# Early second norm, and one up-projection of the next chunk ahead of the output projection, in a fused transformer block

## The chip, the cores and the metric

One Trainium2 chip (trn2), of which the kernel uses one core. The metric is the device time of one execution in microseconds (us). Three executions of the kernel before took 955.98, 957.22 and 959.0 us, median 957.22.

## What is computed

A transformer block with adaptive norms on x of shape 8 x 1024 x 256 (8 rows, 1024 tokens, 256 channels), all in float32:

```python
mod = (silu(c) @ wmod).reshape(8, 6, 1, -1)      # sa, ca, ga, sb, cb, gb; ga and gb kept from small values
h = layernorm(x) * (1 + ca) + sa
x = x + ga * attention(h, W_in, W_out)           # 16 heads of 16; Chebyshev orders 0 to 5 of q and k
h = layernorm(x) * (1 + cb) + sb
x = x + gb * ffn(h)                              # shared expert + 2 of 8 experts, hidden size 128
```

The attention is linear: for each order, the Chebyshev polynomial of k times v is summed over all earlier tokens (a prefix sum), multiplied by the polynomial of q, weighted and added up; the sum is divided by the same quantity without v. The feed-forward computes all 8 routed experts for all tokens and weights each expert's hidden values by its combine weight, sqrt(softplus(logit)) of the two best experts and zero elsewhere; the shared expert has weight one.

## The kernel before

The work is cut into 16 chunks of 512 tokens, two (p = 0, 1) for each of the 8 rows i. It is a software pipeline over 18 steps. In an ordinary step for chunk c, the kernel does the attention of c, the projections (k, q, v) of c+1 (`nxt`), the second norm and the routing of c-1 (`prev`), the experts of c-2 (`exp`), and the first norm's statistics of c+2. Steps 0 and 1 have no experts (step 0 no second norm either); the last four drop parts one by one. Prefix sums are carried from p = 0 to p = 1.

Each engine has its own program, written out by hand in a `step` function; the order of the calls there is the order of execution, and semaphores with fixed counts tie the engines together. Whoever stands in front of a wait holds up all that is behind it on its engine. A "half" is one of six blocks of 128 output columns (k0, k1, q0, q1, v0, v1).

- **TensorE** (L1503): up-projections of the experts (`expert_up`, L1462; 6 matmuls each, in `split_product`, L1368, since weights and inputs are split into a high and a low part), down-projections (`expert_down`, L1487; they add up in `acc`), the six projections of the next chunk, transposes of the norms' results (`transposes`, L1348, matmuls L1359; n = 0 the first norm, n = 1 the second), routing logits (L1394) and their transposes by token (L1402), head sums (L1421), denominators (L1434), the output projection (`project_out`, L1438, matmuls L1445) and, last in the step, the transposes of the combine weights (L1457, L1459). Up-projections and projections go through a ring of two PSUM banks: a group may start when the group two places ahead has been copied out, so for q0 that is k0, and for q1 it is k1. `tr` is two further banks that transposes, head sums and the output projection share.
- **ScalarE** (L863): copies out of the ring, for an expert with a SiLU (`silu(e)`, L845), for k, q and v with a bias (`copy`, L800); `highs` (L781, the high part n1H or n2H from `tr`); the second norm's scaling in four operations (`normalise_second`, L429, operation L435), the squares of the polynomials (L817, L820), `scale_even` (L828, L829), sums for the first norm, the logits' copy (L852) and the copies of the combine weights (L860, L861).
- **VectorE** (L1191): `residual` (L1096, reads `tr`), `token_stats` (L378), `lows` (L961, the low part n1L or n2L from `tr`), the odd orders (L984, L986), `weigh` (the orders times v, L1002 to L1008), `prefix` (scans, L1021), `order_product` (L1042, L1046), `weigh_hidden` (L1169), top-2 and softplus, denominators, `divide` (L1088) and the gated output (L1178).
- **GpSimd** (L738): `inv_std` (ten small operations, L353 to L366, that turn the statistics into scale and shift of the norm), `weigh_order_5` (L653), `scale_wo` (L723, W_out times the row's gate, once per row, at p = 0), additions of orders by accumulating DMAs (L665), two small chains for routing, and the output's DMA (L714).
- **SyncE** (L600): loads, the spread of combine weights and inverse denominators over the partitions by way of DRAM, stores, and the loads of the gates (`load_gate`, L568; 0 the gate of the attention, 1 that of the feed-forward).

In steps without the first norm of the next chunk, and in steps without experts, the calls concerned are left out and the rest keeps its order. The wait ahead of a ring group, in `expert_up` and `project`:

```python
at, bank = use[f"e{e}"]
pe.wait_ge(ring_copied, at - 1)
```

## Time and profile before

| what | value |
|---|---|
| median of 3 runs (lowest, highest) | 957.22 us (955.98, 959.0) |
| the profiled execution: time, span | 953.07 us, 951.3 us |
| TensorE busy (share of the span), instructions | 860.2 us (90%), 4377 |
| TensorE weight loads | 648.6 us (68%), 4377 |
| VectorE | 815.7 us (86%), 1263 |
| ScalarE | 489.8 us (51%), 860 |
| GpSimd | 408.3 us (43%), 502 |
| weightings of hidden values (L1169), 128 | 111.1 us, mean 870 ns |
| mean granted clock of TensorE | 0.964 |

The profiled execution is one of its own, and its 953.07 us are to be set beside its span of 951.3 us; the runs are other executions. "Busy" counts the time in which an engine has an instruction in work. Consecutive matmuls overlap, so a row's own duration is longer than its step to the next row; where the length of a group matters, the starts of two rows are subtracted. The granted clock is the share of TensorE's full clock (2.4 GHz) that it was given. In the rows below PE is TensorE, DVE VectorE, ACT ScalarE, POOL GpSimd. At a row's end, in brackets, stands the idle time ahead of it and what ended it. `x8` is the number of instructions in a row; one matmul in float32 shows as two.

### The profile page before, as it was taken

The page shows a single profiled execution, that of the slowest core. Times are in us where ns is not written, and L with a number is a line of the kernel's source. Part 1 is how long each engine was busy: PE and PEld are TensorE (multiplying, and loading weights), DVE is VectorE, ACT ScalarE, POOL GpSimd, SP SyncE. Part 2 cuts the span into 40 slices and gives each one's busy share as a digit, 9 for nine tenths or more (in the row PEclk, how much of TensorE's full clock was granted, in tenths as well). Part 3 has the DMA queues.
Part 4 walks back from the last instruction along what each step waited for, and adds up shares of the span by engine and source line. Part 5 has one row for each costly group of instructions (what it writes and reads, how often), then busy time and mean ns, then how long its engine had stood idle before and what let it go on. Part 6 is the DMA issues. An engine that isn't in the chain of part 4 may idle for free. (4 is left out here: it accounts for less than half of the span.)

```text
span 951.3 us, 14272 instructions
## 1 busy us (share of the span) xinstructions
PE 860.2 (90%) x4377; PEld 648.6 (68%) x4377; DVE 815.7 (86%) x1263; ACT 489.8 (51%) x860; POOL 408.3 (43%) x502
## 2 busy tenths in 40 slices
PE   5766739999999999999999999999999999979998
PEld 4545427676767676786767676777767676756786
DVE  2696979999989998999989998999999998889423
ACT  4634546555556656655656566566556563441321
POOL 2341444363636355453636254543646253463220
PEclk9975769999999999999999999999999999999999
DMA  8014134453533535453534445354634243443422
GB/s 309 1 29 89 45 68 145 86 153 76 137 92 77 153 79 160 86 155 70 153 77 96 130 87 165 68 155 90 162 71 133 66 100 113 78 133 83 117 79 55
DMA packets 51705, 100.34 MB, mean 105 GB/s; under 512 B 5380, under 2 KB 34127, under 8 KB 49623
## 3 DMA queue, kind: packets, MB, share of 16 engines
q1 hardware_dynamic: 36356, 66.14, 21.2%
q0 software_dynamic: 14832, 33.03, 20.2%
q10 hardware_dynamic: 482, 0.74, 0.2%
q8 instruction: 18, 0.29, 0.1%
q14 instruction: 17, 0.13, 0.0%
HBM read 57.68 MB, written 17.06 MB: 79 GB/s over the span
## 5 line engine op out<-in xcount | busy, mean ns | idle before, releaser
L1487 PE MATMUL acc<-w,hid 128*128 128x256 f32 x1128 | 262.5, 380 | 2.6 <-DVE hid L1169 2.6
L1487 PEld LDWEIGHTS acc<-w,hid 128*128 128x128 f32 x1128 | 213.9, 190 | 37.6 <-DVE hid L1169 4.7
L845 ACT ACTIVATE hid<-ring,b1row 128x512 f32<-128x512 f32 x144 | 98.7, 685 | 143.0 <-PE ring L1368 140.4
L1169 DVE TENSOR_TENSOR hid<-hid,cfw 128x512 f32<-128x512 f32 x128 | 111.1, 870 | 37.0 <-DMA cfw<-cf_rows 21.6
L665 POOL DMA_DIRECT2D feat<-feat x48 | 43.7, 910 | 228.8 <-DVE feat L1046 115.0
L800 ACT ACTIVATE feat<-ring,bqkv 128x512 f32<-128x512 f32 x96 | 65.7, 686 | 81.9 <-PE ring L1368 81.9
L1368 PE MATMUL ring<-n2H,w1H 128*128 128x512 f32 x288 | 102.5, 437 | 0.0
L1445 PE MATMUL tr<-wo_g,feat 128*128 128x256 f32 x256 | 65.3, 413 | 35.9 <-DVE feat L1088 35.9
L1021 DVE TENSOR_TENSOR_SCAN feat<-zero,carry,feat 128x512 f32<-128x512 f32 x80 | 97.1, 1261 | 0.0
L1021 DVE TENSOR_TENSOR_SCAN feat<-zero,feat 128x512 f32<-128x512 f32 x80 | 95.7, 1243 | 0.0
L1368 PE MATMUL ring<-n2H,w1L 128*128 128x512 f32 x288 | 90.8, 397 | 0.0
L1368 PE MATMUL ring<-n2L,w1H 128*128 128x512 f32 x288 | 90.5, 395 | 0.0
L1421 PE MATMUL tr<-feat,const 128*32 128x512 f32 x640 | 89.1, 602 | 0.0
L1445 PEld LDWEIGHTS tr<-wo_g,feat 128*128 128x128 f32 x256 | 51.6, 207 | 49.2 <-DVE feat L1088 33.7
L1368 PE MATMUL ring<-n1H,winH 128*128 128x512 f32 x192 | 69.5, 444 | 15.2 <-issue 7.9
L820 ACT ACTIVATE feat<-feat,const 128x1024 f32<-128x1024 f32 x64 | 70.2, 1142 | 1.0
L353 POOL TENSOR_TENSOR ms<-stats 128x4 f32<-128x4 f32 x18 | 30.2, 1678 | 88.4 <-DVE stats L378 88.4
L1368 PEld LDWEIGHTS ring<-n2H,w1L 128*128 128x128 f32 x288 | 54.4, 189 | 12.7
L1368 PEld LDWEIGHTS ring<-n2L,w1H 128*128 128x128 f32 x288 | 54.5, 189 | 12.5
L1368 PE MATMUL ring<-n1H,winL 128*128 128x512 f32 x192 | 62.8, 409 | 0.0
L1368 PE MATMUL ring<-n1L,winH 128*128 128x512 f32 x192 | 62.8, 409 | 0.0
L1368 PEld LDWEIGHTS ring<-n2H,w1H 128*128 128x128 f32 x288 | 48.8, 191 | 18.5 <-issue 11.7
(171 smaller groups left out, 1559.8 us busy)
## 6 DMA issues: line engine op xcount, KB each, us to landing
feat<-feat POOLq DMA_DIRECT2D x48, 512.0 KB, 4.6
cfw<-cf_rows SPq DMA_DIRECT2D x16, 1280.0 KB, 7.6
xin<-in_L_attn_x SPq DMA_DIRECT2D x16, 512.0 KB, 9.3
feat<-inv_rows SPq DMA_DIRECT2D x32, 256.0 KB
cfw<-cf_rows SPq DMA_DIRECT2D x16, 512.0 KB, 3.6
out<-x SPq DMA_DIRECT2D x15, 512.0 KB, 8.5
out<-fin POOLq DMA_DIRECT2D x15, 512.0 KB, 6.0
cfw<-cf_rows SPq DMA_DIRECT2D x16, 256.0 KB, 4.5
```

Source lines behind the costliest of these rows:

```text
L353: nc.gpsimd.tensor_tensor(t(1), m0, m1, ALU.subtract).then_inc(mv_steps[n], 1)
L665: g.dma_start(f(into), f(of), accum_op=ALU.add).then_inc(added[n], 16)
L800: a.activation(feat[:, (K0 + p, Q0 + p, V0)[m // 2], m % 2], ring[bank][:, :], ACT.Identity, bias=col(bqkv[:, (2, 3, 0, 1, 4, 5)[m]], i)). ...
L820: a.activation(f((qa, qb)[which - 1]), f(s), ACT.Square, bias=cv["biases"][:, which - 1:which]).then_inc(squares, 1)
L845: a.activation(hid[:, e % NG], ring[bank][:, :], ACT.Silu, bias=b1row[:, e:e + 1]).then_inc(ring_copied, 1)
L1021: last = v.tensor_tensor_scan(feat[:, W + n, h], zero[:, 0:1].to_broadcast([P, CT]), feat[:, W + n, h], carry[:, n, h:h + 1] if p else 0.0 ...
L1169: v.tensor_tensor(hid[:, e % NG], hid[:, e % NG], cfw[:, (e - 1) % NW], ALU.mult).then_inc(hidw_ready, 1)
L1368: last = mm(out, w, x, start=(n == 0), stop=(n == len(terms) - 1))
L1421: last = mm(tr[q][g_ * QS:(g_ + 1) * QS, :], cv["headsum"][:, (r // HPH) * QS:(r // HPH + 1) * QS], feat[:, srcs[n], h], start=(n < 4 and ...
L1445: last = mm(tr[t // 2][:, (t % 2) * D:(t % 2 + 1) * D], attn[:, k, t * P:(t + 1) * P], wo_g[:, k], start=(k == 0), stop=(k == KD - 1))
L1487: last = mm(acc[t // 2][:, t % 2], hid[:, e % NG, t * P:(t + 1) * P], w2[:, e], start=False, stop=(e == E), skip_group_check=True)
```

## The change

The second norm of chunk c-1 moves towards the head of the step, on all engines:

- VectorE aggregates its own statistics (`second_mean_var`: four `bn_aggr`, variance plus epsilon, negative mean), and GpSimd has two operations left (`second_inv_std`: power -1/2, product) in place of ten.
- ScalarE normalises in four operations behind n1H and ahead of the SiLUs of experts 1 and 2, takes n2H behind these, and copies q1 apart from k0, k1 and q0, behind the logits.
- TensorE transposes the first norm directly at the step's head (now waiting for the residual's halves one by one), the second norm behind the down-projection of expert 0; the logits stand behind q0, their transposes behind q1, and expert 1 behind that.
- VectorE takes n1L directly behind the aggregations, n2L behind the second weighting, and the third weighting behind the second prefix sum. GpSimd's `weigh_order_5` waits for the second weighting as well.
- The up-projection of the next step's expert 0 stands ahead of the output projection, behind the last down-projection.
- SyncE loads the attention's gate for row i+1 at the end of row i, ahead of the last spread of weights.

```diff
@@ -134,6 +134,7 @@
...
         stats = sb("stats", [P, 2, NT, 6])
+        mean_var = sb("mean_var", [P, NT, 2])
         ms = sb("ms", [P, 2, 12, NT])
@@ -221,6 +222,8 @@
...
         var_steps = sem("variance_steps")
+        aggregate_begun, aggregated, mean_var_ready, second_pow = (
+            sem(f"second_{n}") for n in ("aggregate_begun", "aggregated", "mean_var", "pow"))
         sums_begun, squares_begun, norm_begun = (sem(f"{n}_begun") for n in ("token_sums", "token_squares", "normalisation"))
@@ -378,6 +381,27 @@
...
 
+        def second_mean_var(dve, i, p):
+
+            c = number(i, p)
+            dve.wait_ge(stats_ready[1], c + 1)
+            dve.sem_inc(aggregate_begun, 1)
+            for t in range(NT):
+                last = nc.vector.bn_aggr(mean_var[:, t], stats[:, 1, t])
+            last.then_inc(aggregated, 1)
+            dve.wait_ge(aggregated, c + 1)
+            nc.vector.tensor_scalar(ms[:, 1, 8], mean_var[:, :, 1], EPS_LN, None, ALU.add).then_inc(mean_var_ready, 1)
+            nc.vector.tensor_scalar(ms[:, 1, 10], mean_var[:, :, 0], -1.0, None, ALU.mult).then_inc(mean_var_ready, 1)
+
+        def second_inv_std(pool, i, p):
+
+            c = number(i, p)
+            pool.wait_ge(mean_var_ready, 2 * c + 2)
+            ge(pool, norm_ready[1], c)
+            nc.gpsimd.tensor_tensor(ms[:, 1, 9], ms[:, 1, 8], k_("-half", NT), ALU.pow).then_inc(second_pow, 1)
+            pool.wait_ge(second_pow, c + 1)
+            nc.gpsimd.tensor_tensor(ms[:, 1, 11], ms[:, 1, 10], ms[:, 1, 9], ALU.mult).then_inc(rstd_ready[1], 1)
+
         def token_sums(act, i, p):
@@ -599,9 +623,8 @@
...
                 if p == 0:
-                    if loads or i < B:
-                        ge(sp, wo_ready, i)
-                        load_gate(i, 0)
+                    if i == 0:
+                        load_gate(0, 0)
                     if gb:
@@ -613,6 +636,9 @@
...
                     load(sp, i + 2, p)
+                if p == CB - 1 and i + 1 < B:
+                    sp.wait_ge(wo_ready, i + 1)
+                    load_gate(i + 1, 0)
                 if number(i, p) and number(i, p) <= CB * B:
@@ -650,6 +676,7 @@
...
                 ge(pool, numerator, c)
+                pool.wait_ge(weighted, (ND - 1) * c + 2)
                 g.tensor_tensor(f(W + 4), f(KT5), f(V0), ALU.mult).then_inc(weighted5, 1)
@@ -738,7 +765,7 @@
...
                 if st["second"]:
-                    inv_std(pool, 1, *later(i, p, -1))
+                    second_inv_std(pool, *later(i, p, -1))
                 if st["attn"]:
@@ -874,22 +901,24 @@
...
                 silu(0)
-                silu(1)
                 if qkv:
                     highs(0, *nxt)
+                if second:
+                    for t in range(NT):
+                        normalise_second(act, *prev, t)
+                silu(1)
                 silu(2)
+                if second:
+                    highs(1, *prev)
                 if attn_:
                     scale_even(i, p)
-                for t, half in enumerate(HALVES[:4]):
+                for half in HALVES[:3]:
                     copy(half)
-                    if second:
-                        normalise_second(act, *prev, t)
-                silu(3)
-                if second:
-                    highs(1, *prev)
-                silu(4)
                 if second:
                     copy_logits(*prev)
+                copy("q1")
+                silu(3)
+                silu(4)
                 if st["norm"]:
@@ -1200,27 +1229,25 @@
...
                     token_stats(dve, 1, *prev)
+                    second_mean_var(dve, *prev)
+                if qkv:
+                    lows(0, *nxt)
                 if attn_:
...
                     weigh(i, p, 0)
-                if qkv:
-                    lows(0, *nxt)
+                    weigh(i, p, 1)
+                if second:
+                    lows(1, *prev)
                 if attn_:
-                    weigh(i, p, 1)
                     prefix(i, p, 0)
...
                 expert(1)
-                if attn_:
-                    weigh(i, p, 2)
                 expert(2)
...
                     prefix(i, p, 1)
-                if attn_:
                     carry_over(i, p, 0)
-                if second:
-                    lows(1, *prev)
-                if attn_:
+                    weigh(i, p, 2)
                     order_product(i, p, 0)
@@ -1352,9 +1379,11 @@
...
                     pe.wait_ge(low_ready[0], 2 * (c + 3))
-                else:
-                    ge(pe, x1_ready, 2 * (c - 1 if n == 0 else c + 1))
+                elif n:
+                    pe.wait_ge(x1_ready, 2 * (c + 1))
                 for k in range(KD):
+                    if n == 0:
+                        ge(pe, x1_ready, 2 * (c - 1) - 1 + k)
                     for t in range(NT):
@@ -1500,8 +1529,8 @@
...
 
-            def step(i, p, st):
-                use = ring_of(i, p, st)
+            def step(i, p, st, st_next):
+                use, use_next = ring_of(i, p, st), ring_of(*later(i, p, 1), st_next)
                 nxt, prev, exp = later(i, p, 1), later(i, p, -1), later(i, p, -2)
@@ -1514,29 +1543,29 @@
...
 
-                if ffn:
-                    expert_up(*exp, use, 0)
-                    expert_up(*exp, use, 1)
-                    second_biases(*exp)
                 if isinstance(i, int) and number(i, p) == 0:
...
                     transposes(0, *nxt)
+                if ffn:
+                    expert_up(*exp, use, 1)
+                    second_biases(*exp)
                 expert(0)
-                if qkv:
-                    for half in HALVES[:4]:
-                        project(*nxt, use, half)
-                expert(1)
                 if second:
                     transposes(1, *prev, behind_norm=qkv)
-                expert(2)
+                if qkv:
+                    for half in HALVES[:3]:
+                        project(*nxt, use, half)
                 if second:
                     route_logits(*prev)
+                if qkv:
+                    project(*nxt, use, "q1")
+                if second:
+                    logits_by_token(*prev)
+                expert(1)
+                expert(2)
                 if attn_:
                     head_sums(i, p, 0, second)
-                if second:
-                    logits_by_token(*prev)
-                if attn_:
                     head_sums(i, p, 1, second)
@@ -1551,6 +1580,10 @@
...
                     bias_products()
+                if st_next["ffn"]:
+                    if isinstance(i, int) and number(i, p) == 1:
+                        pe.wait_ge(late_weights, 2)
+                    expert_up(*prev, use_next, 0)
                 if attn_:
@@ -1605,18 +1638,18 @@
...
                 project(0, 0, CHUNK0, half)
-            for i, p, st in FIRST:
-                step(i, p, st)
-            pe.wait_ge(late_weights, 2)
+            def stages(steps, after):
+
+                for n, (i, p, st) in enumerate(steps):
+                    step(i, p, st, steps[n + 1][2] if n + 1 < len(steps) else after)
+
+            stages(FIRST, ALL)
+            pe.wait_ge(s_r2, 4)
             pe.wait_ge(in_w2, 32)
-            pe.wait_ge(s_r2, 4)
-            for p in range(CB):
-                step(1, p, ALL)
+            stages([(1, p, ALL) for p in range(CB)], ALL)
             with pe.Fori(2, B - 1) as i:
-                for p in range(CB):
-                    step(i, p, ALL)
-            for i, p, st in LAST:
-                step(i, p, st)
+                stages([(i, p, ALL) for p in range(CB)], ALL)
+            stages(LAST, some())
 
```

The order of the instructions at three places, of the kernel before and of the changed one. The line numbers of the changed kernel are its own.

TensorE, from the last three down-projections of a step to the head of the next, before:

```order
L1487 MATMUL acc<-w,hid 128x256 x12
L1445 MATMUL tr<-wo_g,feat 128x256 x8
L1457 MATMUL misc<-const,split 128x128
L1459 MATMUL misc<-const,split 64x128 x3
L1368 MATMUL ring<-n2H,w1H 128x512 x2
L1368 MATMUL ring<-n2L,w1H 128x512 x2
L1368 MATMUL ring<-n2H,w1L 128x512 x2
L1368 MATMUL ring<-n2H,w1H 128x512 x2
L1368 MATMUL ring<-n2L,w1H 128x512 x2
L1368 MATMUL ring<-n2H,w1L 128x512 x2
L1476 MATMUL acc<-r,cfR 128x256 x4
L1359 MATMUL tr<-const,ntok 128x128 x8
```

and after:

```order
L1516 MATMUL acc<-w,hid 128x256 x12
L1397 MATMUL ring<-n2H,w1H 128x512 x2
L1397 MATMUL ring<-n2L,w1H 128x512 x2
L1397 MATMUL ring<-n2H,w1L 128x512 x2
L1474 MATMUL tr<-wo_g,feat 128x256 x8
L1486 MATMUL misc<-const,split 128x128
L1488 MATMUL misc<-const,split 64x128 x3
L1388 MATMUL tr<-const,ntok 128x128 x8
L1397 MATMUL ring<-n2H,w1H 128x512 x2
L1397 MATMUL ring<-n2L,w1H 128x512 x2
L1397 MATMUL ring<-n2H,w1L 128x512 x2
L1505 MATMUL acc<-r,cfR 128x256 x4
```

One up-projection (three rows `w1H`, `w1H`, `w1L`) now stands ahead of the output projection (`tr<-wo_g`), and the transposes of the first norm (`ntok`) ahead of the other one.

VectorE, from the residual (`x<-tr,xin`) on, before:

```order
L1096 TENSOR_TENSOR x<-tr,xin 128x512 x2
L378 BN_STATS stats<-x 128x6 x4
L984 SCALAR_TENSOR_TENSOR feat<-feat 128x1024
L986 SCALAR_TENSOR_TENSOR feat<-feat 128x1024
L1002 TENSOR_TENSOR feat<-feat 128x1024
L968 SCALAR_TENSOR_TENSOR n1L<-tr,mods,n1H 128x512 x2
L1004 SCALAR_TENSOR_TENSOR feat<-feat 128x1024
L1021 SCALAR_TENSOR_TENSOR feat<-zero,feat 128x512 x2
L1169 TENSOR_TENSOR hid<-hid,cfw 128x512
L1004 SCALAR_TENSOR_TENSOR feat<-feat 128x1024
L1169 TENSOR_TENSOR hid<-hid,cfw 128x512
L1021 SCALAR_TENSOR_TENSOR feat<-zero,feat 128x512 x2
```

and after:

```order
L1125 TENSOR_TENSOR x<-tr,xin 128x512 x2
L381 BN_STATS stats<-x 128x6 x4
L390 BN_AGGR mean_var<-stats 128x2 x4
L393 TENSOR_SCALAR ms<-mean_var 128x4
L394 TENSOR_SCALAR ms<-mean_var 128x4
L997 SCALAR_TENSOR_TENSOR n1L<-tr,mods,n1H 128x512 x2
L1013 SCALAR_TENSOR_TENSOR feat<-feat 128x1024
L1015 SCALAR_TENSOR_TENSOR feat<-feat 128x1024
L1031 TENSOR_TENSOR feat<-feat 128x1024
L1033 SCALAR_TENSOR_TENSOR feat<-feat 128x1024
L997 SCALAR_TENSOR_TENSOR n2L<-tr,mods,n2H 128x512 x2
L1050 SCALAR_TENSOR_TENSOR feat<-zero,feat 128x512 x2
```

Behind the statistics come six small operations; n1L stands ahead of the odd orders, and n2L ahead of the first scans, where before it stood behind the second.

ScalarE, head of the step (from the SiLU of expert 0 on; `feat<-ring` are the copies of k and q, `ntok` the second norm), before:

```order
L845 ACTIVATE hid<-ring,b1row 128x512 x2
L788 ACTIVATE n1H<-tr,mods 128x512 x2
L845 ACTIVATE hid<-ring,b1row 128x512
L828 ACTIVATE feat<-feat 128x1024
L829 ACTIVATE feat<-feat 128x1024
L800 ACTIVATE feat<-ring,bqkv 128x512
L435 ACTIVATE ntok<-x,ms 128x256
L800 ACTIVATE feat<-ring,bqkv 128x512
L435 ACTIVATE ntok<-x,ms 128x256
L800 ACTIVATE feat<-ring,bqkv 128x512
L435 ACTIVATE ntok<-x,ms 128x256
L800 ACTIVATE feat<-ring,bqkv 128x512
```

and after:

```order
L872 ACTIVATE hid<-ring,b1row 128x512
L815 ACTIVATE n1H<-tr,mods 128x512 x2
L459 ACTIVATE ntok<-x,ms 128x256 x4
L872 ACTIVATE hid<-ring,b1row 128x512 x2
L815 ACTIVATE n2H<-tr,mods 128x512 x2
L855 ACTIVATE feat<-feat 128x1024
L856 ACTIVATE feat<-feat 128x1024
L827 ACTIVATE feat<-ring,bqkv 128x512 x3
L879 ACTIVATE logT<-misc,blog 64x512
L827 ACTIVATE feat<-ring,bqkv 128x512
```

The four operations of the norm stand together, ahead of two SiLUs, n2H, the even scalings (`feat<-feat`) and the copies.

## Rows read from the trace of the kernel before

**Rows 1.** Stretch 3rd to 15th output projection: length, busy us (x) of PE, PEld, DVE, ACT, POOL, clock.
```profile
193.07:826.75 633.68, 611.41 (x3192) 460.97 (x3192) 597.99 (x925) 359.99 (x634) 302.15 (x354) 1.00 0.45 111
```

**Rows 2.** TensorE in order of time: start us, us, what; output projections of three steps.
```profile
456.41 3.72 PE L1445 MATMUL tr<-wo_g,feat 128*128 128x256 f32 x16 [0.98 <-DVE feat L1088]
...
509.78 3.72 PE L1445 MATMUL tr<-wo_g,feat 128*128 128x256 f32 x16 [1.08 <-DVE feat L1088]
...
561.57 3.72 PE L1445 MATMUL tr<-wo_g,feat 128*128 128x256 f32 x16 [0.98 <-DVE feat L1088]
```

**Rows 3.** Who waited for whom: us in total, times, longest us.
```profile
PE tr L1445 <- DVE feat L1088: 35.9, 16, 12.2
DVE n2L L968 <- ACT n2H L788: 24.8, 16, 3.6
PE ring L1368 <- ACT feat L800: 7.2, 6, 1.2
```

**Rows 4.** TensorE in order of time, head of the step that begins at 509.78.
```profile
516.67 0.73 PE L1476 MATMUL acc<-r,cfR 50*128 50x256 f32 x4
...
518.18 0.71 PE L1368 MATMUL ring<-n2H,w1H 128*128 128x512 f32 x2
...
519.65 1.89 PE L1487 MATMUL acc<-w,hid 128*128 128x256 f32 x8
...
521.18 0.81 PE L1368 MATMUL ring<-n1H,winH 128*128 128x512 f32 x2
```

**Rows 5.** ScalarE in order of time.
```profile
515.37 0.69 ACT L845 ACTIVATE hid<-ring,b1row 128x512 f32<-128x512 f32 x1
...
518.13 1.27 ACT L788 ACTIVATE n1H<-tr,mods 128x512 fp32r<-128x512 f32 x2 [0.67 <-PE tr L1359]
...
520.43 1.05 ACT L828 ACTIVATE feat<-feat 128x1024 f32<-128x1024 f32 x1
...
889.52 2.06 ACT L435 ACTIVATE ntok<-x,ms 128x256 f32<-128x256 f32 x4
```

**Rows 6.** GpSimd in order of time, the small operations of the second norm and the two multiplications.
```profile
466.99 3.17 POOL L363 TENSOR_TENSOR ms<-ms,pool_c 128x4 f32<-128x4 f32 x1
...
479.56 1.29 POOL L723 TENSOR_TENSOR wo_g<-wo,gates 128x512 f32<-128x512 f32 x1 [5.02 <-DMA gates<-gate_rows]
...
521.65 1.18 POOL L366 TENSOR_TENSOR ms<-ms 128x4 f32<-128x4 f32 x1
...
522.78 3.42 POOL L653 TENSOR_TENSOR feat<-feat 128x1024 f32<-128x1024 f32 x1
...
886.93 1.04 POOL L363 TENSOR_TENSOR ms<-ms,pool_c 128x4 f32<-128x4 f32 x1
...
888.05 0.20 POOL L365 TENSOR_TENSOR ms<-ms 128x4 f32<-128x4 f32 x1
```

**Rows 7.** VectorE in order of time.
```profile
513.19 1.28 DVE L1096 TENSOR_TENSOR x<-tr,xin 128x512 f32<-128x512 f32 x2
...
514.39 1.39 DVE L378 BATCH_NORM_STATS2 stats<-x 128x6 f32<-128x256 f32 x4
...
523.93 2.83 DVE L1169 TENSOR_TENSOR hid<-hid,cfw 128x512 f32<-128x512 f32 x1
...
531.65 1.41 DVE L968 SCALAR_TENSOR_TENSOR n2L<-tr,mods,n2H 128x512 fp32r<-128x512 f32 x2 [0.78 <-ACT n2H L788]
...
545.15 0.36 DVE L1113 MAX8 top<-route 128x8 f32<-128x8 f32 x4
...
560.18 1.34 DVE L1088 TENSOR_TENSOR feat<-feat 128x512 f32<-128x512 f32 x2 [0.37 <-DMA feat<-inv_rows]
```

**Rows 8.** TensorE in order of time, next to last step.
```profile
892.83 2.00 PE L1487 MATMUL acc<-w,hid 128*128 128x256 f32 x8 [0.82 <-DVE hid L1169]
...
898.47 0.58 PE L1394 MATMUL misc<-n2H,rt 128*64 128x512 f32 x1
...
900.51 0.66 PE L1402 MATMUL misc<-const,logT 128*128 128x128 f32 x4 [0.77 <-ACT logT L852]
```

## The prediction

> **What bounds the kernel now.** I read the stretches first, then the waits, then TensorE's order of time, and last the other engines around the places where TensorE stands. From the output projection of the third chunk to that of the fifteenth, 12 steps take 633.68 us, 52.8 us each, at a granted clock of 1.00; TensorE is busy for 611.41 us of it and VectorE for 597.99 us [rows 1]. So both are nearly full, and a change can win only where TensorE stands or where VectorE is late for it. Two neighbouring steps take 53.37 and 51.79 us from one output projection to the next [rows 2]. TensorE stands at two places. One is ahead of the output projection, for VectorE's division: 35.9 us in 16 waits, some 1.0 us in an ordinary step [rows 2, 3]. The other is ahead of the fourth projection of the next chunk: ScalarE's copy out of the ring is late, because ScalarE itself waits there for the second norm (7.2 us in 6 waits, 1.2 us in each first-half step) [rows 3]. VectorE stands for the second norm's n2H, 24.8 us in 16 waits, 0.78 us in the step shown [rows 3, 7]. It also loses some 2.1 us where GpSimd multiplies order 5: one weighting of the hidden values takes 2.83 us there [rows 6, 7]; 128 of them take 111.1 us in the table above, and with 12 such long ones taken off the others take 0.67.
>
> With its waits taken off, a step of TensorE is 51.79 - 0.98 = 50.8 us, or 53.37 - 1.08 - 1.21 = 51.1 us; I take 50.95. No order can go below that.
>
> **The change, part by part.** P is the start of an output projection.
>
> *The up-projection of expert 0 ahead of the output projection.* It takes 1.5 us, as 519.65 - 518.18 shows [rows 4], and it does nothing new: it fills the 1.0 us in which TensorE stands and takes the same time out of the step's head. The wait at the output projection is then gone if VectorE comes at most 0.4 us later than now. What gets later is everything behind the output projection, by 0.1 to 0.5 us against VectorE.
>
> *The early second norm.* The chain, from P: the second half of the output is there at P+3.6, and VectorE adds the residual until P+4.3 (0.64 for a half) [rows 7]. Statistics: 1.35 us to P+5.65 [rows 7]. Four aggregations are not in the trace. Four MAX8 on equally few elements take 0.36 us, and four statistics over 256 elements take 1.39; I take the lower, since an aggregation reads 6 elements, and keep the upper for the range. With two small operations and two handovers the means are out at P+6.5. GpSimd then has a power and a product, 1.04 and 0.20 us where nothing holds them up [rows 6]: P+7.9. Before, ten operations stood here, and VectorE's between them held them up (one power took 3.17 us) [rows 6]. ScalarE normalises in 2.06 us [rows 5]: P+10.0. Two SiLUs (1.2), two n2H (1.25), two even scalings (2.0) and the copy of k0 (0.65, priced as a SiLU, the same shape) follow on ScalarE [rows 5]: P+15.1.
>
> TensorE meanwhile: projection and routing transposes 3.9 (516.67 - 509.78 less two up-projections of 1.5) [rows 2, 4], biases and transposes of the first norm 1.5 together (the transposes' second half waits for the residual at P+4.3, 0.05), two up-projections of 1.5 and a down-projection of 1.55 [rows 4]: P+10.0. There it is to transpose the second norm, which has just come, 0.1 us late. Then 0.8 for these eight (1.51 less the biases' 0.7), and 3.05 for k0 and k1, two groups as long as an up-projection: P+13.95. The projection q0 needs the ring bank of k0, and that is copied out at P+15.1. **So a new wait of 1.1 us stands ahead of q0, in every step**, for the old one of 1.2 in every second step. In the order of before, four projections followed there with ScalarE free to copy them.
>
> The step becomes 50.95 + 0.1 + 1.1 = 52.15 us, and 12 steps 625.8 instead of 633.7: **-7.9 us**.
>
> *Does VectorE hold?* Now it goes from residual to division in 48.3 us, 560.18 + 1.34 - 513.19 [rows 7]. Off go 0.78 (n2H), 0.37 (inverse) and 2.15 (the multiplication on GpSimd): 45.0. On come 0.7 for the aggregations and small operations and 0.3 for n1H. The multiplication of order 5 now waits for the second weighting and starts with n2L; it holds the SBUF side for 2.3 us (3.42 with 1.2 of waiting) [rows 6], n2L, which reads PSUM, takes 1.4, and the scan behind it waits for the rest, 1.0. Together 47.0, from an effective start at P+3.05: P+50.1, 2 us ahead of TensorE. In a first-half step the gate is already there, since its load is moved to the step before, and the scaling of W_out (1.29) [rows 6] falls upon the scans, where now it lies beside a wait; that step is also 0.4 longer: P+51.8, still 0.3 ahead. VectorE is not the bound, but nearly so.
>
> The Trainium skill ("SBUF — State Buffer", section "SBUF: two separate sides") says that VectorE with two SBUF inputs and a GpSimd operation that reads SBUF take one shared pair of ports as a lock for the whole instruction. By that rule both multiplications move onto scans, which have two SBUF inputs, and the sum above is what it would give; a sum without the rule would put VectorE 1.0 to 2.3 us further ahead and leave the step of TensorE as it is.
>
> *The gate's load* moves from the end of SyncE's queue work at a step's start to the end of the step before, ahead of the last spread of weights. It is one broadcast DMA, issued after the big loads. I cost it at nothing, because the spread behind it waits on SyncE for VectorE's weightings anyway; if that cover were gone, the last spread would be one issue later, and the weightings 7 and 8 that need it come 30 us behind.
>
> *The ends.* In the second step no expert runs and VectorE leads: it loses a wait for n2H, at the mean of 24.8/16 = 1.6 us [rows 3], and 1.1 of the multiplication, and gains 0.7: -2.0. The third step has both the gains and the gate's scaling against them: 0. In the step with chunk 15's attention there is no first norm between statistics and the odd orders, so GpSimd's power starts behind one operation of VectorE; the chain gives n2H some 0.5 us earlier than now: -0.5. In the next to last step TensorE now stands for the weights and goes on at 892.83; behind that come the transposes, 0.8, and the logits, their copy and the transposes by token, 2.45 (898.47 to 900.51 and 0.4) [rows 8]. After the change all of these stand ahead of expert 1. By the chain above the norm is there at 879.69 + 10.0 = 889.7; the two SiLUs and n2H take ScalarE to 892.2, logits, copy and transposes by token go to 895.1, the up-projection of expert 3 to 896.6. So the first down-projection behind the weights comes 3.8 us later, with 0.8 + 2.45 us of work no longer behind it: +0.5. The up-projection of the last chunk stands ahead of the combine transposes, on whose DMA the last step waits: +1.5. Together +2.0.
>
> Sum: -7.9 - 2.0 - 0.5 + 2.0 = -8.4 us, so the ends together are -0.5. On the profiled execution that is 953.07 - 8.4 = 944.7; that execution is 4.15 us below the median of the three runs, 957.22, so against the runs it is 948.8, and I say **949 us**.
>
> **Rivals.**
> 1. *Slower: the norm's small operations on GpSimd are shut out again.* The power and its product have to run while VectorE does n1L, which reads PSUM. That is a window of 1.3 to 1.7 us for 1.04 + 0.20 + two handovers, 1.4 us. If they miss it, they stand behind the odd orders: the power then takes one operation of VectorE more (+0.9), and the product 1.18 instead of 0.20 (+1.0) [rows 6]. For it: those numbers are in the trace, for this very chain. Against it: VectorE waits for n1H there, and so the window opens as soon as the means are out. It decides from 0.65 us onwards, where the wait at q0 passes 1.75 us and the step 52.8. At 1.9 us the step is 54.05: 12 x 1.25 = +15, less 0.5 for the ends: 957.2 + 14.5 = 971.7 us. The Trainium skill's lock (same page and section) is the same mechanism.
> 2. *Faster: the wait at q0 is hidden.* If the chain to k0's copy is 1.1 us shorter than its rows added up, TensorE runs through at 51.05, and VectorE bounds the first-half steps at 51.8: 51.4 on average, 12 x 1.4 = -16.8, less 0.5: 939.9 us. For it: ScalarE's operations overlap by some 0.1 us each. Against it: the adding up already has that.
> 3. *An exchange: the wait only moves.* With aggregations at their upper bound, 1.39 us, the chain is 1.0 us longer, the step 53.15, 12 steps +4.2, less 0.5: 960.9 us at the end of it, and 957 in its middle, where the gain of the filled gap is given back at q0.
>
> **Chances.** The forecast 0.52, rival 1 0.20, rival 2 0.13, rival 3 0.15. A measurement of this kernel tells about 0.3%, 2.9 us, from no change (its three runs lie within 3.0 us). The forecast and rival 2 lie below that, 0.65; rival 3 is half within, half around it; with it stand forecasts whose ends turn out worse: same 0.13; slower 0.22. The range leaves out rival 1: from 937, rival 2 with a bit more overlap, to 962, rival 3 with the aggregations at their bound and 0.1 us of handover per step.
>
> **What would show it.** Right: the wait for VectorE ahead of the output projection is nearly gone, the projection groups wait for ScalarE by 12 to 14 us in 12 or more waits, and VectorE's wait for n2H falls below 6 us; order-5 multiplications of 2.3 to 3.4 us lie beside n2L, and the steps of both halves are within 0.5 us of each other. Wrong: aggregations of over 0.2 us each; a power or product of over 1.1 us; an output projection that still waits for VectorE by 1 us, which says that VectorE is the bound; steps below 51.5 or above 52.8 us.

## The result, and the profile after

The changed kernel takes 948.05 us (median of 6 runs, 946.04 to 950.05), the kernel before 955.63 us (6 runs, 953.91 to 959.0): ratio 0.9909, 95% interval 0.9883 to 0.9935. The ratio is an estimate over all executions and not the quotient of the two medians, which is 0.9921. The forecast was 949 us. The two profiled executions lie nearer to each other than the medians do: 950.05 us (span 948.4) is 2.0 us above its median, 953.07 us (span 951.3) was 2.6 us below. So the spans differ by 2.9 us where the medians differ by 7.6, and what follows counts stretch by stretch.

The stretches of the changed kernel, between output projections and to the end. Columns: length, busy us (x instructions) of PE, PEld, DVE, ACT, POOL, granted clock, DMA share, GB/s:
```profile
140.13:194.33 54.20, 53.38 (x266) 40.01 (x267) 49.87 (x84) 29.90 (x54) 16.34 (x18) 0.96 0.39 103
194.33:818.72 624.39, 613.98 (x3194) 459.86 (x3193) 601.86 (x997) 352.32 (x634) 211.90 (x255) 1.00 0.46 113
818.72:869.37 50.65, 45.57 (x223) 33.09 (x223) 45.92 (x78) 13.08 (x21) 15.23 (x19) 0.90 0.45 106
869.37:948.40 79.03, 68.25 (x294) 55.28 (x294) 24.58 (x61) 18.06 (x29) 9.18 (x13) 0.93 0.29 76
```
The twelve steps take 624.39 us where they took 633.68 [rows 1]: -9.3, 52.0 us each. The other stretches, by the output projections' starts in both traces (before against after): start to the first one, 85.72 and 89.34, +3.6; second step 52.98 and 50.79, -2.2; third 54.37 and 54.20, -0.2; the step with chunk 15's attention 52.94 and 50.65, -2.3; from the last output projection to the end 71.6 and 79.03, **+7.4**. Their sum is -3.0, the difference of the spans but for rounding. Of the 14.0 us that the steps gained, the start and the last stretch took 11.0 back in this execution; how much of that is the run's own shows below.

Who waited for whom in the changed kernel (us in total, times, longest), which answers to [rows 3]:
```profile
PE tr L1474 <- DVE feat L1117: 16.3, 4, 10.0
...
PE ring L1397 <- ACT feat L827: 10.0, 13, 0.9
...
DVE n2L L997 <- ACT n2H L815: 8.2, 4, 5.3
```
The wait ahead of the output projection was 35.9 us in 16 times and is 16.3 in 4, all at the ends; n2H was waited for 24.8 us and is 8.2. In exchange the projection q0 waits in 13 steps, for 0.74 to 0.94 us. TensorE in order of time, the step that answers to the one of [rows 2, 4]:
```profile
507.02 3.72 PE L1474 MATMUL tr<-wo_g,feat 128*128 128x256 f32 x16
...
522.12 0.73 PE L1397 MATMUL ring<-n1H,winH 128*128 128x512 f32 x2 [0.75 <-ACT feat L827]
...
558.82 3.61 PE L1474 MATMUL tr<-wo_g,feat 128*128 128x256 f32 x16
```
Two neighbouring steps took 53.37 and 51.79 us and take 51.95 and 51.80 (455.07 to 507.02 to 558.82): **the whole gain of these steps is in those that also scale the output weights (the long ones, every second); the others have not moved.**

The norm's chain in that step, in order along the chain (VectorE, GpSimd, ScalarE), then GpSimd's order 5, n2L, the first scan and the division, to be set beside [rows 5 to 7]; P is again the start of the step's output projection, here 507.02:
```profile
513.05 0.38 DVE L390 BATCH_NORM_AGGREGATE mean_var<-stats 128x2 f32<-128x6 f32 x4 [0.15 <-DVE stats L381]
...
513.80 1.03 POOL L401 TENSOR_TENSOR ms<-ms,pool_c 128x4 f32<-128x4 f32 x1 [3.53 <-DVE ms L394]
...
514.90 0.20 POOL L403 TENSOR_TENSOR ms<-ms 128x4 f32<-128x4 f32 x1
...
515.23 2.08 ACT L459 ACTIVATE ntok<-x,ms 128x256 f32<-128x256 f32 x4 [1.01 <-POOL ms L403]
...
520.27 2.39 POOL L680 TENSOR_TENSOR feat<-feat 128x1024 f32<-128x1024 f32 x1 [5.16 <-DVE feat L1033]
...
520.01 1.41 DVE L997 SCALAR_TENSOR_TENSOR n2L<-tr,mods,n2H 128x512 fp32r<-128x512 f32 x2
...
521.33 3.59 DVE L1050 TENSOR_TENSOR_SCAN feat<-zero,carry,feat 128x512 f32<-128x512 f32 x2
...
556.98 1.34 DVE L1117 TENSOR_TENSOR feat<-feat 128x512 f32<-128x512 f32 x2 [0.62 <-DMA feat<-inv_rows]
```
The four aggregations take 0.38 us, the power 1.03 and the product 0.20, nothing shut out; the norm starts at P+8.2 (forecast P+7.9) and q0 waits 0.75 us (forecast 1.1). The order-5 product now lies beside n2L and the first scan, which takes 3.59 us; the division waits for the inverse, 0.62 us, and is done at 558.32, P+51.3, half a microsecond before TensorE comes.

### The profile page after: what moved, and what is told of

It is laid out like the page before. It is cut to its first block and busy times, and to the rows that moved or that the text cites. A ratio compares the mean times of both kernels' runs of the same rounds, so it can differ in the third digit from the quotient of the medians.

```text
span 948.4 us, 14215 instructions
## 1 busy us (share of the span) xinstructions
PE 864.7 (91%) x4377; PEld 649.7 (69%) x4377; DVE 819.1 (86%) x1359; ACT 480.6 (51%) x860; POOL 296.8 (31%) x374
## 5 line engine op out<-in xcount | busy, mean ns | idle before, releaser
L872 ACT ACTIVATE hid<-ring,b1row 128x512 f32<-128x512 f32 x144 | 96.3, 680 | 187.9 <-PE ring L1397 187.9
L1198 DVE TENSOR_TENSOR hid<-hid,cfw 128x512 f32<-128x512 f32 x128 | 87.1, 690 | 38.2 <-ACT hid L872 24.4
L1397 PE MATMUL ring<-n2H,w1H 128*128 128x512 f32 x288 | 109.9, 463 | 0.0
L1050 DVE TENSOR_TENSOR_SCAN feat<-zero,feat 128x512 f32<-128x512 f32 x80 | 108.3, 1402 | 0.0
L1050 DVE TENSOR_TENSOR_SCAN feat<-zero,carry,feat 128x512 f32<-128x512 f32 x80 | 103.3, 1341 | 0.0
L1450 PE MATMUL tr<-feat,const 128*32 128x512 f32 x640 | 85.5, 596 | 0.0
L1474 PE MATMUL tr<-wo_g,feat 128*128 128x256 f32 x256 | 63.0, 402 | 16.4 <-DVE feat L1117 16.3
L680 POOL TENSOR_TENSOR feat<-feat 128x1024 f32<-128x1024 f32 x16 | 39.0, 2436 | 84.7 <-DVE feat L1033 84.7
```

The lines of the kernel that those rows point to most:

```text
L680: g.tensor_tensor(f(W + 4), f(KT5), f(V0), ALU.mult).then_inc(weighted5, 1)
L872: a.activation(hid[:, e % NG], ring[bank][:, :], ACT.Silu, bias=b1row[:, e:e + 1]).then_inc(ring_copied, 1)
L1050: last = v.tensor_tensor_scan(feat[:, W + n, h], zero[:, 0:1].to_broadcast([P, CT]), feat[:, W + n, h], carry[:, n, h:h + 1] if p else 0.0 ...
L1198: v.tensor_tensor(hid[:, e % NG], hid[:, e % NG], cfw[:, (e - 1) % NW], ALU.mult).then_inc(hidw_ready, 1)
L1397: last = mm(out, w, x, start=(n == 0), stop=(n == len(terms) - 1))
L1450: last = mm(tr[q][g_ * QS:(g_ + 1) * QS, :], cv["headsum"][:, (r // HPH) * QS:(r // HPH + 1) * QS], feat[:, srcs[n], h], start=(n < 4 and ...
```

## The experiments

All were run beside the kernel before, in three groups, each on one chip. The kernel before had medians of 957.62, 962.26 and 954.22 us in them, so kernels of different groups are compared by their ratio to it. The changed kernel itself was run in none of the three; its ratio is that of the section before. Like there, a ratio is an estimate over all executions and can differ from the quotient of two medians, by up to 0.002 here. The steps come from one profiled execution of each kernel. "Long" and "short" are the medians of five steps each, of those with and without the scaling of the output weights, from the output projections' starts; "last" is from the last output projection to the end.

| kernel | ratio (95% interval) | long | short | 12 steps | last |
|---|---|---|---|---|---|
| before | 1 | 53.56 | 51.79 | 633.7 | 71.6 |
| changed | 0.9909 (0.9883 to 0.9935) | 52.01 | 51.80 | 624.4 | 79.0 |
| group 1: e0_at_head | 0.9888 (0.9851 to 0.9924) | 52.50 | 51.55 | 625.0 | 75.9 |
| e0_alone | 1.0004 (0.9979 to 1.0030) | 53.85 | 51.38 | 634.9 | 75.3 |
| ten_ops | 1.0315 (1.0277 to 1.0352) | 54.69 | 54.62 | 654.8 | 77.8 |
| even_later | 0.9891 (0.9848 to 0.9935) | 52.15 | 51.35 | 622.5 | 76.0 |
| group 2: vector_more | 0.9902 (0.9876 to 0.9929) | 52.60 | 51.91 | 630.4 | 77.3 |
| tensor_more | 0.9970 (0.9948 to 0.9992) | 52.71 | 52.51 | 632.0 | 78.8 |
| order5_free | 0.9996 (0.9972 to 1.0021) | 53.07 | 52.27 | 635.1 | 76.9 |
| gate_load_back | 0.9906 (0.9874 to 0.9937) | 52.33 | 52.39 | 628.1 | 76.5 |
| group 3: step0_order | 0.9892 (0.9861 to 0.9924) | 51.99 | 51.81 | 623.7 | 77.2 |
| tail_as_before | 0.9878 (0.9853 to 0.9903) | 51.94 | 51.82 | 623.5 | 73.8 |
| both_ends | 0.9849 (0.9820 to 0.9878) | 51.98 | 51.80 | 623.4 | 73.4 |
| ends_and_even | 0.9822 (0.9790 to 0.9854) | 52.07 | 51.25 | 621.8 | 71.9 |

### The up-projection ahead: undone, and alone

`e0_at_head`, against the changed kernel (TensorE's step):
```diff
+                if ffn:
...
+                    expert_up(*exp, use, 0)
                 if qkv:
                     transposes(0, *nxt)
...
-                if st_next["ffn"]:
...
-                    expert_up(*prev, use_next, 0)
                 if attn_:
                     project_out(i, p)
```


> Changed kernel, but the up-projection of the shared expert stands at the head of the step again (ahead of the first norm's transposes); the early second norm stays. Theory 1 (the step of the prediction: it fills a gap of 1.0 us ahead of the output projection, TensorE sets the step): the gap comes back in every steady step, +1.0 us x 12 and some at the ends, 960 to 963 us. Theory 2 (VectorE and the norm's chain set the step: with the up-projection at the head, the 0.75 us wait ahead of q0 is hidden behind it, and the gap returns for it): about +0.1 to +0.6 us a step, 949 to 956 us, wait ahead of q0 near 0, wait ahead of the output projection 0.8 to 1.5 us.

`e0_alone` is the kernel before with the reverse edit and nothing else.

> Kernel before, and of the change only the up-projection of the shared expert ahead of the output projection. Theory 1 (TensorE sets the step of the kernel before, and 1.0 us of it is the gap): 1.0 us less in each of 12 steps, 942 to 945 us. Theory 2 (VectorE sets it: the earlier head finds VectorE no earlier, and the gap moves to another wait): within 2 us of the kernel before, 953 to 956 us, with longer waits for low parts or hidden rows on TensorE.

Undone: ratio 0.9888. Alone: 1.0004, with some 2.5 us either way in its interval, where 12 us were to be won. The move is worth nothing that can be measured, in either company. The rows say why. TensorE in `e0_at_head`, a long step's end and the wait ahead of q0 behind it:
```profile
508.45 3.71 PE L1474 MATMUL tr<-wo_g,feat 128*128 128x256 f32 x16 [1.02 <-DVE feat L1117]
...
524.62 0.74 PE L1397 MATMUL ring<-n1H,winH 128*128 128x512 f32 x2 [0.68 <-ACT feat L827]
```
The gap is back (1.02 us), but in long steps only, and q0 waits 0.68 us as well; short steps are 0.25 us shorter, long ones 0.5 longer. Next, VectorE's n2L in a long step of the kernel before, and then in `e0_alone` the same with TensorE's output projection at the step's end:
```profile
479.76 1.41 DVE L968 SCALAR_TENSOR_TENSOR n2L<-tr,mods,n2H 128x512 fp32r<-128x512 f32 x2 [2.22 <-ACT n2H L788]
```
```profile
477.90 1.41 DVE L968 SCALAR_TENSOR_TENSOR n2L<-tr,mods,n2H 128x512 fp32r<-128x512 f32 x2 [2.21 <-ACT n2H L788]
...
508.42 3.72 PE L1445 MATMUL tr<-wo_g,feat 128*128 128x256 f32 x16 [0.19 <-DVE feat L1088]
```
The gap is filled, 0.19 us instead of 1.08 [rows 2], and the long steps are no shorter (53.85 against 53.56): the output projection comes when VectorE has divided, and VectorE still stands 2.21 us for n2H. TensorE's wait moved ahead of the fourth projection, 1.8 us in long steps instead of 1.2 [rows 3]. (Short steps did become 0.4 us shorter, 51.38, and VectorE's wait for n2H in them fell from 0.8 to 0.24 us; the long ones took it back.) **The gap was TensorE being early, not time to be won.** Theory 2 holds in both, but for one of its signs: the wait ahead of q0 did not go to 0 in `e0_at_head`. In the forecast's sum the filled gap was the wrong term.

A number that needs no list of waits shows the same for any of the kernels: the time from the end of VectorE's division to the start of the output projection, which is 0.04 to 0.14 us in all steps of the kernel before, where TensorE was there first, and more when it was not. It is worked out from start and duration of the two rows, for the steps that end between 299 and 820 us:

| kernel | ends of five long steps | ends of five short steps |
|---|---|---|
| before | 0.13 to 0.14 | 0.04 to 0.05 |
| e0_alone | 0.12 to 0.13 | 0.05 to 0.23 |
| changed | 0.13 | 0.33 to 0.73 |
| e0_at_head | 0.12 to 0.14 | 0.05 to 0.32 |

Before, VectorE's division released every step, behind the waits that VectorE itself had. In the changed kernel it releases the long steps, and TensorE comes last in the short ones. In the long ones it is close: the last rows of TensorE ahead of 507.02 start 0.46 us apart, the last of them at 506.52, so that it can have stood 0.04 us at most. Which of the two would give way needs the edits further below.

### The ten operations in the new place

`ten_ops`: the changed kernel without `second_mean_var`, and `inv_std(pool, 1, ...)` for `second_inv_std`.

> Changed kernel with the ten GpSimd operations of the old inverse deviation in place of VectorE's aggregation and GpSimd's two, in the new early place. The ten took 6.96 us in the kernel before (515.87 to 522.83) beside odd orders. Theory 1 (the norm chain is what the transposes at P+10.5 wait for): the norm starts some 4.5 to 5 us later, TensorE waits 4 to 4.5 us more in each step with a second norm, 998 to 1010 us. Theory 2 (slack behind the norm, or the operations run faster where no odd order is beside them): 2 us a step or less, below 976 us.

Ratio 1.0315, 4.1% above the changed kernel, some 39 us; steps of 54.6 to 54.7, 2.7 to 2.8 us more each. Theory 1 by its mechanism, at two thirds of its size. GpSimd's operations in one step (starting at 527.15), then the norm on ScalarE and the transposes on TensorE:
```profile
533.01 0.20 POOL L356 TENSOR_TENSOR ms<-stats 128x4 f32<-128x4 f32 x1 [3.56 <-DVE stats L381]
...
534.40 1.04 POOL L366 TENSOR_TENSOR ms<-ms,pool_c 128x4 f32<-128x4 f32 x1
...
535.52 0.89 POOL L368 TENSOR_TENSOR ms<-ms 128x4 f32<-128x4 f32 x1
...
536.37 1.18 POOL L369 TENSOR_TENSOR ms<-ms 128x4 f32<-128x4 f32 x1
...
537.68 2.08 ACT L459 ACTIVATE ntok<-x,ms 128x256 f32<-128x256 f32 x4 [3.43 <-POOL ms L369]
...
539.88 1.95 PE L1387 MATMUL tr<-const,ntok 128*128 128x128 f32 x8 [2.17 <-ACT ntok L459]
```
The first eight run beside n1L (533.82 to 535.2) or beside nothing, 0.20 us the small ones; the last two lie beside odd orders and take 0.89 and 1.18. So the norm starts at P+10.5, 2.3 us behind the changed kernel's, and TensorE waits 2.17 us for it. Behind that wait its granted clock falls, though the kernel is in the middle of its steady steps (the third figure from the end):
```profile
539.88:544.00 4.12, 4.12 (x15) 0.59 0.99 330
544.00:549.00 5.00, 5.00 (x22) 1.00 0.21 58
```
The eight transposes then take 1.95 us, where the changed kernel has 1.04. So it is, more or less, in ten of the twelve steps; in the two others the same wait of 2.16 and 2.17 us left the clock up, and these steps were 0.5 us shorter (54.1). The early place needs the short chain: with the old ten operations in it the kernel would be 3% slower than before.

### Which engine sets the step

`even_later`, ScalarE:
```diff
+                copy("k0")
+                copy("k1")
                 if attn_:
                     scale_even(i, p)
-                for half in HALVES[:3]:
-                    copy(half)
+                copy("q0")
```


> Changed kernel with ScalarE's two scalings of the even orders behind the copies of k0 and k1 and ahead of that of q0. Theory 1 (TensorE sets every step and the 0.75 us wait ahead of q0 is pure loss): the wait goes to 0 and 0.75 us x 12 go, 938 to 941 us. Theory 2 (VectorE's divide is only 0.5 us ahead of the output projection, so it becomes the bound): 0.3 to 0.5 us a step, 943 to 946 us, and waits of 0.2 to 0.5 us come up ahead of the output projection. Theory 3 (the copies were not held by the scalings): 948 us.

The wait ahead of q0 is gone. Two neighbouring steps, long and short (columns as above):
```profile
450.57:502.62 52.05, 51.53 (x267) 38.31 (x267) 50.84 (x86) 29.89 (x54) 17.95 (x22) 1.00 0.46 117
502.62:553.84 51.22, 51.02 (x267) 38.44 (x267) 49.72 (x82) 29.86 (x55) 18.03 (x23) 1.00 0.46 114
```
Short steps lose 0.45 us, long ones nothing (52.15 against 52.01), and now the output projection follows the division by 0.05 to 0.25 us in both kinds: VectorE sets both, or is within some 0.2 us of doing so. The 7 runs reach from 942.9 to 952.67 us, so the ratio, 0.9891, does not tell theory 2 from theory 3. The steps speak for theory 2; they are those of the fastest of the 7, but the same edit on other ends (`ends_and_even`, below) shows the same: short steps of 51.25 us against 51.80, long ones unchanged.

`vector_more`, VectorE, and `tensor_more`, TensorE:
```diff
+                if q:
+                    ge(dve, extra, number(i, p))
+                    v.scalar_tensor_tensor(out=pad[:, :], in0=const[:, 0:384], scalar=0.0, in1=const[:, 0:384], op0=ALU.add, op1=ALU.mult).then_inc(extra, 1)
```
```diff
                 pe.wait_ge(ring_copied, at - 1)
+                if e == E:
+                    for n in range(3):
+                        mm(ring[bank][:, :], w1H[:, e, 0], n2H[:, p, 0], start=(n == 0), stop=(n == 2))
```


> Changed kernel with one operation more on VectorE behind the clips in each step (a product of constants of 384 columns into a buffer that nothing reads; by the 1.22 us of such an operation on 1024 columns about 0.46 to 0.5 us), nothing else waits for it. Theory 1 (VectorE's chain sets the step): +0.5 us in each of 12 steady steps and some at the ends, 953 to 956 us. Theory 2 (TensorE sets it, as the prediction's sum of the changed step had it, VectorE 0.5 us or more ahead): 948 to 949 us. Both bind in turn: about +0.25 us a step, 951 us.

> Changed kernel with three matmuls of 512 columns more ahead of the last expert's up-projection in each step (0.23 us each, 0.70 us a step; they write a bank that is started afresh behind them). Theory 1 (TensorE sets the step): +0.70 us in each of 12 steady steps and 1.4 to 2.8 us at the ends, 957.5 to 960 us. Theory 2 (VectorE's chain sets it): 0 to 0.2 us a steady step, 949 to 952 us.

The added operation on VectorE stands ahead of the second clip (that of q), not behind both, and starts 0.47 us before the one behind it. VectorE: ratio 0.9902, no measurable difference. TensorE: 0.9970, 6 us more, its interval apart from the changed kernel's; that lies between its two theories (theory 1 asks for 9.5 us or more). By the steps, 0.70 us on TensorE makes both kinds 0.7 us longer (52.51, 52.71); why the long ones too isn't shown. Half a microsecond on VectorE shows in long steps (52.60 against 52.01), and hardly in short ones (51.91; three of the five are within 0.11 of 51.8).

These medians are good to some 0.3 us only, since in this group several kernels had steps of 53.1 to 53.5 us among the ordinary ones. The rows tell which wait grows there. VectorE's division in two short steps of `vector_more`, of 53.53 and 51.79 us:
```profile
350.57 1.29 DVE L1122 TENSOR_TENSOR feat<-feat 128x512 f32<-128x512 f32 x2 [2.77 <-DMA feat<-inv_rows]
...
664.00 1.34 DVE L1122 TENSOR_TENSOR feat<-feat 128x512 f32<-128x512 f32 x2 [0.33 <-DMA feat<-inv_rows]
```
VectorE waits for the DMA that spreads the inverse denominators. In `vector_more` and `gate_load_back` the long steps of 52.8 us and more have waits of 0.8 to 1.3 us there, the other long ones 0.2 to 0.6; the short steps of 52.4 us and more have 1.5 to 2.8, the other short ones 0.3 to 1.1. Beside `gate_load_back`, the nearest kernel to the changed one on that chip (52.33 and 52.39), the added half microsecond can't be seen at all. So `vector_more` decides little: its ratio is that of theory 2, and the 0.3% of "both bind in turn" lie at the edge of what the two intervals leave. What carries the reading is `even_later` and `ends_and_even`, where less on TensorE's path shortens the short steps alone, and the table of the division's ends: **short steps are TensorE's, long ones VectorE's** (with its DMA), and each has the other within half a microsecond.

### GpSimd's added wait, and the gate's load

`order5_free` takes the line `pool.wait_ge(weighted, (ND - 1) * c + 2)` out of `weigh_order_5`.

> Changed kernel without GpSimd's added wait ahead of its product of order 5, which then runs beside VectorE's odd and even orders instead of beside the low parts of the second norm and the first scan (that scan took 3.59 us beside it, 2.45 us alone). Theory 1 (VectorE sets the step and the place of the product only moves the collision): the first scan is back at 2.33 to 2.45 us, but the operations at P+8 to P+12 lose the same, 946.5 to 950 us. Theory 2 (the wait protects the chain to the low parts of the second norm: without it the product of 2.4 to 3.4 us shuts those operations out and TensorE waits for them): 0.5 to 1.2 us a step slower, 954 to 962 us. Theory 3 (the collision was pure loss): 1.1 us a step faster on VectorE, 0.3 of it seen, 943 to 945 us.

Ratio 0.9996: the whole gain is gone, as theory 2 had it in size (some 8 us more). GpSimd's product, and VectorE's orders beside it, in a long step:
```profile
575.26 3.44 POOL L679 TENSOR_TENSOR feat<-feat 128x1024 f32<-128x1024 f32 x1
...
575.26 1.22 DVE L1012 SCALAR_TENSOR_TENSOR feat<-feat 128x1024 f32<-128x1024 f32 x1
...
576.39 3.39 DVE L1014 SCALAR_TENSOR_TENSOR feat<-feat 128x1024 f32<-128x1024 f32 x1
...
579.71 1.21 DVE L1030 TENSOR_TENSOR feat<-feat 128x1024 f32<-128x1024 f32 x1
```
The product starts right behind the norm's small operations and shuts one odd order out: 3.39 us instead of 1.21. n2L, and with it the scan and all behind it, come that much later, and 1.1 us of it remain in a long step, 0.5 in a short one. The first scan is back at 2.32 to 2.45 us, as theory 1 said, but what the orders lose is more than that. It is VectorE that is late (the output projection follows its division by 0.05 to 0.22 us in both kinds), not TensorE that waits for n2L. Beside n2L and the scan the same product costs 1.1 us (3.59 instead of 2.45). The Trainium skill ("SBUF — State Buffer", section "SBUF: two separate sides") lets a VectorE operation with two SBUF inputs and a GpSimd one that reads SBUF take turns at a shared pair of ports; these rows and those of the ten operations agree: 0.20 us beside n1L, which reads PSUM, 0.89 and 1.18 beside odd orders.

`gate_load_back` puts `load_gate(i, 0)` back to the head of SyncE's step.

> Changed kernel with the load of the output projection's gate back at its old place in SyncE's queue. The prediction priced the move at nothing. In the changed kernel GpSimd's scaling of the output weights waits 3.95 us for that load and then runs beside the second scan in every second step (3.38 us instead of 2.33). Theory 1 (the move matters nowhere): 947 to 949 us, the scaling some 4 us later, beside other VectorE work. Theory 2 (the scaling's new place costs VectorE 1 us in every second step and the old one does not): 2 to 6 us faster, 942 to 946 us. Theory 3 (the earlier load helps): 2 us slower or more.

Ratio 0.9906: theory 1, no difference from the changed kernel; the two intervals together leave some 4 us either way. The scaling waits 7.9 us for its gate instead of 3.95 and starts 4 us later, as expected.

### The two ends

`step0_order`, VectorE:
```diff
-                if qkv:
+                if qkv and second:
                     lows(0, *nxt)
                 if attn_:
                     odd(i, p, 1)
                     weigh(i, p, 0)
+                if qkv and not second:
+                    lows(0, *nxt)
+                if attn_:
                     weigh(i, p, 1)
```


> Changed kernel with VectorE's old order in step 0 alone, which has no second norm: the low parts of the next chunk's first norm behind the odd orders and the first weighing. Times of this chip against the kernel before: the changed kernel has 0.9909. Theory 1 (step 0 lost its 3.6 us to VectorE's wait of 4.66 us for the high parts): output projection of chunk 0 at 84.5 to 87 us instead of 86.5 to 90.4, 2.5 to 3.6 us less in all, ratio 0.987 to 0.9885. Theory 2 (the start differs from run to run by as much, 84.5 to 90.4 us over the profiles so far, and loads set it): no change, ratio 0.990 to 0.992.

In step 0 there is no second norm, and VectorE used to have the odd orders to do while the next chunk's high parts were made. The low parts in the changed kernel, and in `step0_order`:
```profile
44.30 1.60 DVE L997 SCALAR_TENSOR_TENSOR n1L<-tr,mods,n1H 128x512 fp32r<-128x512 f32 x2 [4.66 <-ACT n1H L815]
```
```profile
45.49 1.60 DVE L997 SCALAR_TENSOR_TENSOR n1L<-tr,mods,n1H 128x512 fp32r<-128x512 f32 x2 [0.36 <-ACT n1H L815]
```
When the first transposes of that step start varies between profiles by 5 us (39.5 to 44.9), which no order in the step can cause. From there to the output projection the time is steady: 42.9 us in both kernels with the old order, 46.8 to 47.1 in eight with the new one (45.2 in `order5_free`), 43.4 to 43.6 in the three with this edit. So the edit gives 3.4 us back in the trace. The ratio, 0.9892, lies between the two theories and has both in its interval; the output projection of chunk 0, at 87.02 us, tells as little, since the start moves by more.

`tail_as_before`: in steps without attention, TensorE's second transposes stand behind expert 1 and the logits behind expert 2 again, ScalarE's and VectorE's parts to match; and
```diff
-                if st_next["ffn"]:
+                if st_next["ffn"] and attn_:
...
                     expert_up(*prev, use_next, 0)
                 if attn_:
                     project_out(i, p)
                 if second:
                     combine_by_expert(*prev, attn_)
+                if st_next["ffn"] and not attn_:
+                    expert_up(*prev, use_next, 0)
```


> Changed kernel with the old order in the steps without attention (the second norm's transposes behind expert 1, the logits behind expert 2, ScalarE and VectorE to match) and the up-projection of the last chunk's shared expert behind the combine weights' transposes. Theory 1 (the 7.4 us that the stretch from the last output projection to the end is longer than before come from these places: TensorE waits 0.58, 2.12 and 0.77 us, its clock falls behind them, and 1.59 us of up-projection stand ahead of the combine weights): that stretch 71.5 to 74 us instead of 79.0, ratio 0.983 to 0.986. Theory 2 (only the waits themselves, 3.5 us, and the 1.59 us come back, the clock stays low): 74 to 76 us, ratio 0.986 to 0.989. Theory 3 (the end is set by the spread of the combine weights and the last hidden rows, whichever order): 77 us or more, ratio 0.989 to 0.991.

Ratio 0.9878, the last stretch 73.8 us: theory 1's 71.5 to 74 is met by the stretch, theory 2's 0.986 to 0.989 by the ratio. The 79.0 of the changed kernel's profile is the longest of its kind: the other eight kernels without this edit that have the new norm have 75.9 to 78.8 (some with edits of their own in it). By the median of these nine, 77.2, against the one profile of before (71.6), 5.5 us of the 7.4 are the order's, and 3.4 came back (2 to 5 by the range). The last stretch of the changed kernel on TensorE, then two eighths of it with the granted clock (the third figure from the end):
```profile
869.37 3.72 PE L1474 MATMUL tr<-wo_g,feat 128*128 128x256 f32 x16 [0.65 <-DVE feat L1117]
...
882.70 0.66 PE L1423 MATMUL misc<-n2H,rt 128*64 128x512 f32 x1 [2.12 <-ACT n2H L815]
...
886.18 1.20 PE L1397 MATMUL ring<-n2H,w1H 128*128 128x512 f32 x2
...
911.02 0.27 PE L1486 MATMUL misc<-const,split 128*128 128x128 f32 x1
...
921.53 2.47 PE L1516 MATMUL acc<-w,hid 128*128 128x256 f32 x8 [3.15 <-DVE hid L1198]
```
```profile
879.25:889.13 9.88, 6.75 (x24) 0.65 0.57 208
889.13:899.01 9.88, 9.88 (x46) 1.00 0.05 8
```
The transposes and logits that now stand ahead of expert 1 find no cover in a step without projections: TensorE waits 0.58, 2.12 and 0.77 us for the norm, n2H and the logits' copy, and the clock falls to 0.65 on average. Six matmuls of expert 3's up-projection then take 2.66 us (886.18 to 888.84), where 1.5 is their time. Without those waits in front, in `tail_as_before`:
```profile
866.73 3.72 PE L1483 MATMUL tr<-wo_g,feat 128*128 128x256 f32 x16 [0.47 <-DVE feat L1124]
...
880.38 3.51 PE L1525 MATMUL acc<-w,hid 128*128 128x256 f32 x8 [2.73 <-DVE hid L1205]
...
889.60 0.66 PE L1440 MATMUL misc<-const,logT 128*128 128x128 f32 x4 [0.78 <-ACT logT L879]
```
It waits 2.73 us for the weights once. The clock falls behind that wait as well (0.54 over 880.38 to 883.73: eight down-projections take 3.35 us, where it is 1.5 at full clock) but is back at 1.00 behind them. From the last output projection to the combine weights it is P+39.3, against P+41.65 and P+37.2 before. The part behind the combine weights (911.02 to the end) takes 37.4 us in the changed kernel and 36.8 in `e0_alone`, but 34.4 before and 34.5 in `e0_at_head` and here: the up-projection ahead of the weights' transposes delays their DMA by its 1.6 us and then is missing as cover while TensorE waits for what hangs on it (3.15 us at 921.53, and 0.41 in the same place before).

> The two edits before together. Theory 1 (both ends were what the prediction lacked, and they add): the first stretch 2.5 to 3.6 us shorter and the last 5 to 7.4 us, ratio 0.980 to 0.983. Theory 2 (only the last stretch is real): the ratio of the kernel with the old tail alone, within 0.001.

> Both ends as before, and ScalarE's scalings of the even orders behind the copies of k0 and k1. Theory 1 (in steps without a scaling of the output weights TensorE is the bound and the 0.75 us ahead of q0 is loss; in the others VectorE binds at the same time): 0.45 us less in every second step, 2 to 3.5 us less than the kernel with both ends alone, ratio 0.977 to 0.981. Theory 2 (VectorE binds everywhere as soon as the wait goes): the ratio of both ends alone, within 0.001.

Both ends: 0.9849, short of theory 1 (0.980 to 0.983) and beyond theory 2 (0.9868 to 0.9888), each of which is partly in its interval. It is 0.003 from the old tail alone, with overlapping intervals, so that the two add is likely and not shown; its interval is apart from the changed kernel's. With the later scalings: 0.9822, **936.05 us against 954.22**, the best version measured, short steps 51.25 us and a last stretch of 71.9. Theory 1 asked for 0.977 to 0.981, theory 2 for 0.9839 to 0.9859; the ratio lies between, and its interval overlaps with that of both ends alone. The short steps say theory 1, 0.55 us less for the 0.45 forecast.

## Why the prediction was right, and where it was not

*The total.* -8.4 us forecast, -7.6 measured (955.63 to 948.05); 949 against 948.05 us. The two parts behind it: twelve steps -7.9 forecast, -9.3 in the trace; the ends -0.5 forecast, +6.3 in that trace (3.6 - 2.2 - 0.2 - 2.3 + 7.4). With the last stretch at its usual +5.5 the ends are +4.4; the medians would leave +1.7 for them, and one profile of the kernel before can't settle which. Either way the steps gained more than forecast and the ends lost what the forecast had as a small gain, and the one error made good a part of the other: that the total is right within 1 us is in part luck.

*The chain to q0.* In pairs of the form "0.36 for 0.38" the forecast comes first and the measured value second. The aggregation at the lower bound (0.36 for 0.38), the power and product open (1.04 + 0.20 for 1.03 + 0.20), a new wait ahead of q0 (1.1 for 0.75): right in kind and nearly in size. Rival 1 (shut-out operations) did not come, since VectorE was at n1L; `ten_ops` and `order5_free` show that it would have: each puts GpSimd's work beside odd orders and loses the gain or more. Rival 2 is what `even_later` made true: with the wait gone the steps are 51.35 and 52.15 us, 51.75 on average and not 51.4, with VectorE as the bound. Rival 3 needed aggregations near 1.39 us. Of the forecast's signs, the waits ahead of q0 came in 13 steps but add up to 10.0 us and not 12 to 14, and VectorE's wait for n2H is 8.2 us and not below 6, 5.3 of it in the next to last step alone; the place of the order-5 product and the likeness of the two kinds of steps are as forecast.

*The filled gap failed.* "It fills the 1.0 us in which TensorE stands" is true and gave nothing (1.0004 alone, 0.9888 undone). The sum took TensorE's waits off the step, as if VectorE were ahead of it. It was not: the long steps of before were VectorE's, with 2.2 us of standing for n2H in them (the 479.76 row above), and the gap was its shadow. The early norm took that standing away, and the long steps went from 53.56 to 52.01 us, where VectorE still sets the step. But the standing is not all of it. The rows of VectorE in one long step, of the kernel before and then of the changed one, where it is held up by GpSimd's product (the first row of each) and, in the changed one, by the scaling (the last row):
```profile
472.42 2.67 DVE L1169 TENSOR_TENSOR hid<-hid,cfw 128x512 f32<-128x512 f32 x1 [0.26 <-DMA cfw<-cf_rows]
475.01 2.33 DVE L1021 TENSOR_TENSOR_SCAN feat<-zero,feat 128x512 f32<-128x512 f32 x2
```
```profile
468.93 3.51 DVE L1050 TENSOR_TENSOR_SCAN feat<-zero,feat 128x512 f32<-128x512 f32 x2
...
473.55 3.38 DVE L1050 TENSOR_TENSOR_SCAN feat<-zero,feat 128x512 f32<-128x512 f32 x2
```
Such a step adds up so: 2.2 us of standing less; 0.8 less beside the order-5 product (2.0 at a weighting before, 2.67 for 0.67; 1.2 at the first scan now, 3.51 for 2.33); 1.05 more for the scaling beside the second scan (3.38 for 2.33); 0.75 more for aggregations and small operations; 0.25 more for the residual. That is -1.0, as its step from one gated output to the next went from 53.3 to 52.3; the other 0.4 is the lead that it brings along from the short step. The product's place is as needed as the norm's: without it the whole gain is gone (`order5_free`). In short steps VectorE gained too (0.78 us of standing; `even_later` brings 0.45 of it out), but TensorE's new wait of 0.75 us took its place. The forecast treated long and short steps alike, at 52.8 and 52.15 us; the right mean came from the wrong halves, which is luck.

*VectorE near the bound.* For a long step the sum had P+51.8 and 0.3 us to spare; VectorE came at P+51.8 and TensorE had been there, so it was the bound after all. For a short step P+50.1 was 1.2 us too early (558.32 is P+51.3).

*The ends.* Second step -2.0 for -2.2, third 0 for -0.2. The step with chunk 15's attention -0.5 for -2.3: VectorE's wait for n2H there fell from 3.57 to 1.65 us, and the output projection at its head took 3.56 us (818.72 to the next row, behind a wait of 0.16, clock 1.00) instead of 5.25 (826.75, behind one of 2.07, clock 0.67). Step 0 was not in the sum at all, and the runs show +4.0 us from its transposes on. The last stretch was put at +2.0 and is about +5.5: the sum had the order right (though its 895.1 is 0.45 us later than the terms it names, 892.2 + 2.45), but neither the clock that falls when the new places wait nor the lost cover behind the combine weights.

## What to carry over

A gap on one engine is worth its length only if what it waits for could come earlier; put the candidate in alone, and look which wait takes its place. Where steps alternate, make the sum for each kind, since a wait that binds in one can be free in the other. A reordering made for the steady step has to be costed again in the first and last steps, where the work that covered it is missing: here the start and the last stretch cost 11.0 us in the profiled execution, more than the twelve steps gained, and giving them their old order took the kernel from 0.9909 to 0.9849.

## What the hardware showed that was not expected

- The granted clock falls behind some waits of 2 us and more, in steady steps too: 0.59 over 4.1 us behind a wait of 2.17 us in `ten_ops`, 0.67 over an output projection of the kernel before behind 2.07 us, 0.65 over 9.9 us of the changed kernel's last stretch, and 1.00 in the next. Logits matmuls of 512 columns start 0.42 to 0.46 us apart there, the lower of the two levels (1.2 GHz), against 0.23 at the upper one. The length of the wait doesn't decide it alone: waits of 2.16 and 2.17 us in two steps of `ten_ops`, and one of 2.35 us ahead of the last output projection of the kernel before (879.69), left the clock at 1.00. Nor did waits of 0.82 and 0.77 us lower it in the next to last step of before. What decides isn't shown.
- One product on GpSimd of 2.3 to 3.4 us costs VectorE 2.2 us beside an odd order and 1.1 us beside n2L and a scan; where it starts is worth the whole change.
- Steps of 53 us among steps of 52 come and go in the same kernel, on one chip more than on others. In the changed kernels they go with VectorE's wait for the DMA of the inverse denominators (2.77 us in a short step of 53.53 us, 0.33 in one of 51.79); what makes that DMA late stays open.
